# A new order of events for the attention part of a one-layer language-model tower on one core

## What is computed

```python
h = _L0_tok_ref(x, ...)                                   # hashed embedding of 4 x 512 tokens, layer norm, width 192
h = h + _L0_attn_ref(_layernorm(h), qkv_w, ...)           # two attentions in a row, 12 heads of 16
h = h + _L0_ffn_ref(_layernorm(h), gate_w, w1, ...)       # 8 experts, the best 2 of them for each token
...
attn = softmax(einsum('bnd,bmd->bnm', q, k) * scale)      # first attention
out = einsum('bnm,bmd->bnd', attn, v)
out = out @ proj_w.T + proj_b
sim_tokens = out / maximum(norm(out), EPS)                # second attention: similarity of the first one's output
sim = einsum('bnd,bmd->bnm', sim_tokens, sim_tokens) * 10.0
sim = where(sim < 0, -inf, sim)
out2 = einsum('bnm,bmd->bnd', softmax(sim), v)
out2 = out2 @ proj_w.T + proj_b
```

## Time and profile before

| | us |
|---|---|
| median of 3 runs | 600.11 |
| lowest and highest run | 595.86, 603.89 |
| the profiled execution, its own time | 599.07 |
| span from its first to its last instruction | 597.3 |
| PE busy, DVE busy, ACT busy, POOL busy | 527.5, 428.8, 336.5, 226.8 |
| mean granted TensorE clock, as a share of 2.4 GHz | 0.959 |

### The profile page before, as it was taken

One profiled execution on the slowest core, in us unless ns is written; L12 is line 12 of the kernel. 1 busy time (PEld: TensorE's weight loads), 2 busy tenths in 40 slices (PEclk: granted clock), 3 DMA queues, 4 the chain that ended last, 5 costly groups with the idle time before them and its releaser, 6 DMA issues.

```text
span 597.3 us, 11968 instructions
## 1 busy us (share of the span) xinstructions
PE 527.5 (88%) x3532; PEld 322.8 (54%) x3533; DVE 428.8 (72%) x927; ACT 336.5 (56%) x790; POOL 226.8 (38%) x282
## 2 busy tenths in 40 slices
PE   0548899999999999999997987879999999999991
PEld 0223333443344323534253333568998999999990
DVE  3579997989898999897679999965775444434420
ACT  1223676768797888788977876215332424433430
POOL 6891221426151341102322320032455665656442
PEclk9979899999999999999998999868999999999996
DMA  4271142146442345321222659195232343333321
GB/s 118 61 128 32 37 72 45 41 69 115 52 71 56 57 67 76 42 66 47 63 49 86 87 115 289 43 314 189 33 52 44 57 62 49 47 60 47 45 29 20
DMA packets 42252, 45.24 MB, mean 76 GB/s; under 512 B 10419, under 2 KB 37045, under 8 KB 42198
## 3 DMA queue, kind: packets, MB, share of 16 engines
q0 software_dynamic: 12864, 19.97, 19.8%
q1 hardware_dynamic: 29334, 24.62, 18.0%
HBM read 17.88 MB, written 7.70 MB: 43 GB/s over the span
## 4 chain that ended last, share of the span: by engine, by line
PE 63%; DVE 19%; issue 6%; POOL 5%; ACT 3%; DMA 2%; DVEq 0%; POOLq 0%; ACTq 0%
PE psum L1400 12%; PE psum L1541 11%; PE psum L1518 8%; DVE MX L1187 6%; PE psum L1461 5%; PE psum L1468 5%; PE psum L1453 5%; PE psum L1525 4%; PE psum L1490 4%; DVE arena L1201 3%; POOL H L668 3%; PE psum L1425 2%; PE psum L1437 2%; ACT arena L828 2%; DMA result<-T,slot_dest 1%
## 5 line engine op out<-in xcount | busy, mean ns | idle before, releaser
L828 ACT ACTIVATE arena<-psum 128x512 f32<-128x512 f32 x384 | 205.1, 615 | 42.5 <-PE psum L1468 21.3
L1187 DVE TENSOR_REDUCE MX<-psum 128x1 f32<-128x512 f32 x192 | 123.3, 681 | 12.1 <-PE psum L1453 11.3
L1201 DVE SCALAR_TENSOR_TENSOR arena<-arena 128x1024 f32<-128x1024 f32 x96 | 117.1, 1241 | 10.3 <-ACT arena L828 10.1
L1400 PE MATMUL psum<-arena 128*17 128x512 f32 x768 | 102.9, 608 | 4.5 <-DVE arena L1201 3.1
L730 POOL DMA_INDIRECT result<-T,slot_dest x39 | 64.8, 1662 | 62.3 <-DVE T L1317 60.1
L573 POOL DMA_DIRECT2D KS<-arena x72 | 36.9, 514 | 112.1 <-PE psum L1468 53.7
L1468 PE MATMUL psum<-KS,QS 96*128 96x512 bf16 x192 | 66.3, 388 | 1.0 <-ACT arena L828 0.9
L712 POOL DMA_INDIRECT xg_sb<-x_rows,slot_token x39 | 40.1, 1028 | 69.4 <-DVE slot_token L1122 38.0
L861 ACT ACTIVATE arena<-psum,b_sb 128x128 f32<-128x128 f32 x120 | 32.2, 398 | 58.4 <-PE psum L1525 58.4
L1453 PE MATMUL psum<-late_stacks,arena 96*128 96x512 bf16 x144 | 51.6, 400 | 11.0 <-DMA late_stacks<-arena 7.6
L1518 PE MATMUL psum<-O,arena 128*128 128x128 f32 x468 | 58.9, 284 | 2.0 <-DVE O L942 1.3
(11 more groups left out here) (223 smaller groups left out, 759.7 us busy)
## 6 DMA issues: line engine op xcount, KB each, us to landing
late_stacks<-arena POOLq DMA_DIRECT2D x72, 64.0 KB, 3.7
QS<-arena SPq DMA_DIRECT2D x72, 64.0 KB, 3.6
KS<-arena POOLq DMA_DIRECT2D x72, 64.0 KB, 3.8
arena<-w SPq DMA_DIRECT2D x8, 576.0 KB, 9.3
arena<-arena SPq DMA_DIRECT2D x54, 64.0 KB, 3.6
arena<-w SPq DMA_DIRECT2D x8, 384.0 KB, 7.6
x_rows<-X SPq DMA_DIRECT2D x4, 384.0 KB, 3.9
result<-H SPq DMA_DIRECT2D x4, 384.0 KB, 5.0
```

Source lines behind the costliest of these rows:

```text
L828: act.activation((P1, P2)[ps][:, n % PRING, :], s, ACT.Exp, scale=(QSCALE, SIM_SCALE)[ps]).then_inc(done, 1)
L1187: dve.tensor_reduce(MX[:, g % 2, CT * i + c:CT * i + c + 1], slot(k), AX_X, ALU.max).then_inc(freed[k % RING], 1)
L1201: dve.scalar_tensor_tensor(p, p, 1.0, p, ALU.is_ge, ALU.mult).then_inc(masked, 1)
L1400: last = pe.matmul(acc[ps][32 * i:32 * i + VW, :], V[b][:, c, GH * (g % GB) + i, :], (P1, P2)[ps][:, n % PRING, :], start=c == 0, stop=c = ...
```

## The change

The table `PLACE` is replaced by another one. The events, their instructions, tiles, waits and shapes stay the same; 1150 places are assigned anew. Counted by engine, the relative order differs for 270 of PE's 789 events (by 11 positions at most), 187 of ACT's 524 (6), 102 of DVE's 416 (6), 35 of POOL's 162 (8) and 26 of SP's 161 (3). From place 1085 to the end of the list three events change their order. The waits of `keep_clock` name the next PSUM event instead of `normalise` of the last group; with either table these are the same event.

The diff, cut to the lines that are spoken of below:

```diff
     ('embed_norm', 'centre'): (
-        3, 34, 82, 233),
+        3, 13, 82, 233),
+    ('embed_norm', 'affine'): (
+        4, 25, 98, 240),
+    ('attn_stats', 'stats'): (
+        5, 31, 103, 263),
...
     ('attn_norm',): (
-        13, 45, 175, 341),
...
+        9, 39, 169, 339),
...
     ('mid', 'c_proj'): (
-        40, 89, 241, 432),
+        30, 87, 243, 430),
...
     ('save', 1): (
-        465, 571, 656, 737, 818, 877, 944, 980, 1017, 1059, 1101, 1138),
+        464, 568, 656, 736, 817, 878, 944, 981, 1022, 1068, 1102, 1138),
     ('normalise', 1): (
-        499, 584, 670, 765, 839, 895, 950, 997, 1029, 1104, 1115, 1133),
+        491, 584, 672, 765, 838, 896, 950, 999, 1029, 1105, 1117, 1133),
...
     ('out_norm', 'moments'): (
-        729, 931, 1055, 1145),
+        721, 930, 1059, 1146),
...
     ('route',): (
-        1088, 1092, 1106, 1117, 1118, 1120, 1125, 1129, 1131, 1132, 1134, 1135, 1136, 1137, 1139, 1146, 1149),
+        1088, 1091, 1106, 1116, 1118, 1120, 1125, 1129, 1131, 1132, 1134, 1135, 1136, 1137, 1139, 1145, 1149),
...
                         if (g, c, ps) == (NG - 1, CT - 2, 1):
-                            wait_consumed(pe, unit("normalise", NG - 1, 1) - RING)
-                            keep_clock(slot(unit("normalise", NG - 1, 1)), MASK_TURNS)
+                            wait_consumed(pe, k + 1 - RING)
+                            keep_clock(slot(k + 1), MASK_TURNS)
```

More of the change, by code:

```diff
@@ L154 @@
     ('embed_norm', 'stats'): (
-        0, 10, 60, 179),
+        0, 8, 59, 191),
     ('embed_norm', 'moments'): (
-        1, 16, 65, 207),
+        1, 11, 65, 212),
     ('embed_norm', 'rstd'): (
-        2, 27, 72, 231),
+        2, 12, 80, 230),
     ('embed_norm', 'centre'): (
-        3, 34, 82, 233),
-    ('load_qk',): (
[4 rows of a table removed]
[L167 to L172, removed]
@@ L173 @@
-    ('attn_stats', 'rstd'): (
-        11, 44, 148, 272),
-    ('attn_norm',): (
-        13, 45, 175, 341),
-    ('x_transpose',): (
-        14, 18, 53, 64, 205, 212, 350, 353),
+        3, 13, 82, 233),
[3 more added lines that the diff above has]
+        5, 31, 103, 263),
+    ('attn_stats', 'moments'): (
+        6, 34, 123, 272),
+    ('attn_stats', 'rstd'): (
+        7, 35, 135, 285),
+    ('attn_norm',): (
+        9, 39, 169, 339),
+    ('x_transpose',): (
+        10, 14, 51, 60, 206, 211, 351, 353),
@@ L179 @@
+    ('load_qk',): (
[4 rows of a table added]
     ('q_proj',): (
-        24, 67, 218, 398),
+        17, 66, 218, 400),
     ('mid', 'q_proj'): (
-        26, 74, 224, 420),
+        19, 72, 224, 419),
     ('k_proj',): (
-        33, 71, 222, 413),
+        21, 71, 222, 410),
     ('c_proj',): (
-        35, 80, 234, 424),
+        23, 78, 234, 428),
     ('mid', 'k_proj'): (
-        36, 78, 226, 422),
+        26, 76, 226, 421),
+    ('mid', 'c_proj'): (
+        30, 87, 243, 430),
     ('v_proj',): (
-        39, 43, 84, 92, 242, 249, 509, 521),
@@ L191 @@
-    ('mid', 'c_proj'): (
-        40, 89, 241, 432),
+        37, 38, 84, 91, 237, 245, 509, 521),
     ('max_unit',): (
[9 rows of a table removed]
[9 rows of a table added]
     ('max_row',): (
-        70, 115, 164, 216, 268, 326, 389, 489, 557, 650, 734, 819),
+        70, 112, 162, 215, 268, 325, 390, 492, 560, 651, 733, 820),
     ('exp_unit',): (
[9 rows of a table removed]
[9 rows of a table added]
     ('pv', 0): (
[3 rows of a table removed]
[3 rows of a table added]
     ('save', 0): (
-        142, 191, 243, 298, 361, 439, 534, 614, 705, 782, 860, 915),
+        142, 188, 244, 296, 359, 439, 531, 626, 702, 781, 856, 911),
     ('normalise', 0): (
-        159, 198, 250, 312, 370, 446, 540, 631, 711, 803, 875, 917),
+        161, 199, 251, 313, 369, 446, 543, 632, 714, 803, 879, 917),
@@ L223 @@
     ('o_transpose', 0): (
-        261, 264, 456, 458, 719, 726, 922, 924),
+        262, 264, 461, 463, 729, 737, 924, 926),
     ('proj_norm',): (
-        277, 281, 472, 485, 747, 750, 938, 946),
+        273, 277, 472, 483, 747, 750, 938, 945),
     ('unit_tokens', 'squares'): (
-        283, 488, 751, 945),
+        281, 488, 753, 946),
     ('unit_tokens', 'rstd'): (
-        294, 498, 761, 947),
+        291, 503, 763, 948),
     ('unit_tokens', 'scale'): (
-        306, 531, 788, 951),
+        304, 529, 786, 951),
@@ L265 @@
     ('normalise', 1): (
[L266 removed]
+        491, 584, 672, 765, 838, 896, 950, 999, 1029, 1105, 1117, 1133),
     ('o_transpose', 1): (
[L268 removed]
+        677, 700, 906, 908, 1035, 1039, 1140, 1141),
     ('proj_out',): (
[L270 removed]
+        709, 716, 913, 915, 1045, 1047, 1142, 1143),
     ('out_norm', 'stats'): (
[L272 removed]
+        718, 921, 1055, 1144),
```

15 lines of the change are left out of this document (6 added, 9 removed), and 94 rows, old and new, of the table PLACE.

## The result

The changed kernel takes 601.68 us (median of 12 runs, 597.79 to 605.37), the kernel before 597.86 (12 runs beside it, 595.86 to 603.89; the three runs shown ahead of the prediction are among them). The ratio is 1.0071, interval 1.005 to 1.0091. So it is slower by 0.7%, well under 2%, where 597.1 us and a small gain were forecast. The number lies in the range and the likeliest class, within 2%, came; the sign of the change was wrong.

The account below looks back on a forecast made before the run. PE (63% of the chain) and DVE (19%) were taken to bound the kernel, loads hardly ever. From 599.07 us, -0.4 - 1.0 - 0.3 - 0.3 = -2.0 gave 597.1 us, range 592.5 to 603.5 (the forecast case's own: 595.5 to 598.5).

Parts of the forecast that it names:

- Start, 0: Up to the first score product at 41.92 us: the moved DVE and POOL work costs nothing, 0 us.
- wrong if the first product comes later than 42.5: Sign at the first score product: expected to stay at 41.9 us; later than 42.5 would refute the prediction.
- 62 to 72 us, -0.4: Three reductions ahead of DVE's affine let PE's held-back product start earlier: -0.4 us, bounds 0 and -0.7.
- 84 to 93 us, -1.0: Seven reductions between DVE's attn_norm(2) and stats of batch 3 shorten PE's waits: -1.0 us, bounds 0 and -1.27.
- behind this place PE sets the pace: Step of the 84 to 93 us term: DVE, idle 8.7 of 73 us from 67 to 140, can catch up.
- the stalls only move: Rival: a stall removed comes up at the next long DVE block; only -0.6 or nothing remains, 599.3 us; chance 0.3.
- 353 to 359 us, -0.3: ACT's save three exponentials later removes DVE's wait of 0.31 us: -0.3 us, bounds 0 and -0.6.
- 397 to 399.5 us, -0.3: DVE copies the first token block before moments, so the experts start earlier: -0.3 us, bounds 0 and -0.4.
- The other swaps, 0 within 2: Remaining moves of exponentials or reductions by one or two products, mostly where PE is never idle: 0, bounds -2 and +2.
- The loads, 0: No load becomes late after 41.92 us; tightest is load_sim(3,5) behind load_qk(11,0), cover 2.5 us, 0.7 under load: 0 us.
- The sum: Whole kernel: the four gains, -0.4, -1.0, -0.3 and -0.3, make -2.0 us, from 599.07 to 597.1.
- change of the experts' stretch by more than 1 us: Sign in the stretch behind the attention: 197.8 us should remain; a change above 1 us would refute the prediction.

Follow-up runs that it names:

- a2: The changed kernel unaltered, run once more for a second trace only; first score product at 41.04 us.
- a3: The changed kernel unaltered, timed again on chip B against the kernel before: ratio 1.0015.
- u_rstd3: Changed kernel with only ACT's rstd of batch 1 moved back behind the mid of q_proj(0), third timing, chip D: ratio 0.9992 to the kernel before.
- u_mid: Changed kernel with only mid of c_proj(1) two events later, so POOL's L564 follows DVE's centre of batch 2; chip C: ratio 1.006 to the kernel before.
- b2: The kernel before unaltered, run once more for a second trace, the base of trace comparisons; span 594.7 us.
- p3: p2 plus the change's two late moves, save(9,1) later and route take ahead of the out_norm moments of batch 3: ratio 0.9972 to the kernel before.
- p4: p3 with the gathers of batch 2 between POOL's third and fourth memset of the stacks: ratio 0.9951 to the kernel before.
- old_new: Old order for the first 323 events, new order behind (from near 133 us): ratio 1.0003 to the kernel before.
- a4: The changed kernel unaltered, timed a third time, on chip C, against the kernel before: ratio 1.0073.
- p_before: Kernel before, event order unchanged, with POOL's gathers of batches 2 and 3 moved behind its constants; chip D: ratio 1.0058.
- p2: Kernel before with POOL's constants and later gathers moved back and DVE's centre of batch 1 right behind the moments of batch 1: ratio 0.9956.
- u_rstd: Changed kernel with only ACT's rstd of batch 1 moved back behind the mid of q_proj(0), chip A: ratio 1.0001 to the kernel before.
- u_rstd2: Same kernel as u_rstd, timed beside the changed kernel itself on chip B: ratio 1.0022 to the kernel before.
- o_rstd2: Kernel before with only ACT's rstd of batch 1 moved right behind x_transpose(0,0), second timing, chip E: ratio 0.9989.

## Why the prediction was right or wrong

**Start, 0: the step that failed.** The term priced DVE's `centre` and `affine` and POOL's low part of `c_proj(0)`. It left out one moved event, ACT's `rstd` of batch 1, which now stood ahead of a copy that everything waits for. It looked free: in the old trace ACT is idle there and the moments are done at 22.0. With the early signal it is free (first product in a2 and a3 41.04 and 41.06). With the late one it costs 1.7 to 3.2 us at the first product (43.05, 43.62, 44.57 against 41.33 in u_rstd3), and this is what the traces show between 1.007 and 1.0015. The rule that I gave myself, "wrong if the first product comes later than 42.5", caught it. In the first trace of the changed kernel PE's transposes also start 1.26 us late (21.70 instead of 20.44), which in no other trace of this order happened. It is a late signal too: the norm apply that they wait for ended at 20.34, as elsewhere, and was signalled at 21.56.

**62 to 72 us, -0.4: wrong, +0.92.** The reordering by itself did what the sum said of it at first: against its own first product PE is 0.92 us ahead at `pv(0,0,0)` in eight traces of the new order (1.84 in u_mid, near the 1.8 of the sum), and gives it back at `max_unit(2,1,0)` (1.08) and `max_row(1)` (1.03). Two steps failed. The gain itself: u_mid, without the collision, gives back all of its 1.84 us by `max_row(1)`, so the move is worth 0 and not -0.4; DVE sets the pace and has no less to do. And the cover by an unchanged duration: DVE was already 0.92 late by the collision at 60 us, just ahead of the stretch that I had read. No row of before shows `centre` beside an L564, and I took an unchanged duration for granted.

**84 to 93 us, -1.0: wrong, about -0.1.** The step that failed is "behind this place PE sets the pace". I read it from the stretch of 67 to 140 us, where DVE is idle for 8.7 of 73 us. From 80 to 90 us alone DVE is busy for 9.45 of 10 in b2 and in a3. From 74 to 94 us its reductions in a3, start taken off, keep a constant distance to b2 (0.90 to 0.92 us, where no event is swapped). That is the rival "the stalls only move", which had 0.3. Another 0.5 us was gained up to 114 us in the traces of the new order; 0.39 of it is a wait of PE ahead of `max_unit(4,7,0)`, where in the old order a refinement (L918) lies beside an L564 and takes 1.03 us instead of 0.16.

**353 to 359 us, -0.3: right.** From `pv(9,2,1)` to `pv(10,2,1)` the new order wins 0.4 us in every trace that has it, and p3 and p4 win the same by the one move of `save(9,1)`. PE's wait for the tokens of batch 2 falls from 1.48 to 1.18 us:

```profile
362.45 1.05 PE L1425 MATMUL psum<-ident,X 128*96 128x128 f32 x8 [1.18 <-DVE X L923]
```

**397 to 399.5 us, -0.3: right.** The copy now precedes the moments, as the row says, and the first expert product comes 7.76 us behind `proj_out(3,0)` in old_new, where the traces of before have 8.07:

```profile
402.45 0.42 DVE L942 COPY O<-psum 128x256 f32<-128x256 f32 x1
402.79 0.37 DVE L912 BATCH_NORM_AGGREGATE mv<-stats_out 128x2 f32<-128x6 f32 x4
```

**The other swaps, 0 within 2: right in size.** Up to 285 us they win some 0.5 to 0.6 where the clock holds. But in five of nine traces with the new order behind 133 us the clock falls at 281 to 286 us (0.83 in the stretch of 280 to 290 us of the changed kernel, a4 and u_rstd3), and in none of the eleven with the old one. Where it does, PE loses 1.5 to 1.6 us there:

```profile
280.00:290.00 10.00, 10.00 (x63) 3.56 (x55) 5.54 (x8) 7.72 (x16) 2.70 (x4) 0.83 0.16 48
```

Those five do not have the fall near 317 to 322 us that the other four have, and from 263 to 348 us they lose 1.2 to 1.3 us against b2, the four others 0.2 to 1.0, the kernel before 0.6 (the eleven traces with the old order 0 to 1.1).

**The loads, 0: right.** Behind the first product PE waits for none of them. The tightest one, `load_sim(3,5)` behind `load_qk(11,0)`, was issued at 216.39 us in the changed kernel and landed 3.0 us later, at 219.42; `sim_unit(3,0,0)` read it at 222.32. So the cover was 2.9 us, and the 5.6 us under load that the prediction weighed did not come up there.

**The sum.** With the early signal it is +0.92 at 60 us, -0.6 up to 114, -0.4 and -0.3 at the end, and between 263 and 348 us -0.5 to +0.7 against the kernel before; where the clock falls near 70 us, the new order pays 0.5 more for it. That makes -0.9 to +0.8 us; 1.0015 is +0.9, and its interval holds no change at all. With the late signal 1.7 to 3.2 us come on top. 1.0071 is 4.2 us, which a start of 3.2 and the upper end of the rest, together 4.0, nearly reach. a4's 1.0073 is 4.4 us, and its start was only 1.7 later, so some 2 us of that loss stay without a place. The forecast had -2.0. Its sign of a change of the experts' stretch by more than 1 us could tell nothing, since that stretch, untouched, varies by more from trace to trace (last section).

That the number, 601.68, lies in the range of 592.5 to 603.5 is the width of the range, not the working: of the four gains in the sum only the last two, -0.3 each, came.

## What to carry to other kernels

A table that moves hundreds of events is priced event by event on the path, on every engine: the one small instruction set ahead of a copy that all wait for counts for more than all the blocks of DVE. "Done by then" in one trace is a cover only as long as the signal is in time, and one trace doesn't tell that of another; a wait that can come late goes behind what everybody needs. When a block of DVE or POOL moves, look at what the other of the two does in SBUF at the new place, and ask of a stall which engine is busy in these ten microseconds, not in the hundred around them.

## What the runs showed of the hardware that I had not expected

- **DVE and POOL in SBUF.** Beside POOL's L564 (1.15 us, it reads and writes SBUF) a DVE instruction that has all its operands in SBUF doesn't get done before L564 has ended. In the twenty traces nine of nine instructions of `centre` that start beside an L564 take 1.33 us instead of 0.41, and twelve of twelve L918 take 1.02 to 1.10 instead of 0.16. A mask (L1201, 1.22 us) that starts beside one can end 1.08 us behind it and so take up to 2.19. It goes the other way too: an L564 that starts behind a mask ends 1.0 us behind it and takes up to 2.4 us. Instructions that read PSUM do not stretch: none of 370 reductions beside an L564 does, and in p4 thirteen of them take the 7.86 us of the earlier trace rows beside an L564 and all of POOL's constants. Beside POOL's memset that writes two partitions the norm apply stretches, from 1.25 to 2.5 us in p_before, p2 and p3, but none of 24 instructions of `centre`, whose four in a3 took 1.40 us as always. Beside POOL's gathers nothing stretches by more than 0.12 us. One thing stays open: in u_rstd, u_rstd2 and u_rstd3 a short step of 0.16 us near 37 us took 0.87 to 1.08 us with only loads of POOL (L573) beside it, while 88 of 91 such steps beside such loads did not stretch.
- **A signal that comes late.** The end of DVE's moments of batch 1 is signalled at once in all traces of chips A, B, E and F, and 2.9 to 3.8 us later in all four of chip C and in u_rstd3 on D. In p_before, also on chip D, no gathers lie beside it, and the signal came at once (23.37, instruction ended at 23.36). That points to the gathers, but it is one trace; on chip F (p4) gathers lie beside it and it is in time. Chip and hour can't be told apart, since each chip had one group of runs. What holds it back stays open.
- **The clock.** After the pauses of PE near 62 to 70 us the granted clock falls part of the time to its lower level, 1.2 GHz, in some executions of one and the same kernel and not in others: 0.83 in the stretch of 62 to 72 us of the first trace of the kernel before, 1.00 in b2. It costs 0.8 to 1.1 us in the old order and 1.5 to 1.6 in the new one; in o_rstd2, of the old order, with 0.69 in the stretch of 62 to 72 us, it cost 2.3. The experts' stretch, untouched in all kernels, varied between 195.0 and 199.6 us. So a single trace can't price a change of half a microsecond by its span, but the offset of an event between two falls can.
